# A window-ratio kernel on one core: its band matmuls split over the contraction into two of 64 rows on two row tiles

## What is computed

```python
def box_sum(x, axis, w): ...   # sum over a window of w, zero padded (w//2 before, w-w//2-1 behind)

v = _gn(x)                                    # (x - mean) / sqrt(var + 1e-5), 32 groups
s = box_sum(v, 2, 5)                          # 5 along the width
num = box_sum(s * s, 3, 20)                   # 20 along the channels
d = box_sum(box_sum(v * v, 2, 5), 3, 20)
norm = c1[None, :]                            # how many of the 5 lie inside
out = x + nan_to_num(num / (d * norm), nan=1.0)
```

## Time and profile before

| | |
|---|---|
| median of 2 runs | 423.67 us (423.52 to 423.82) |
| the profiled execution, its own time | 425.8 us |
| its span in the trace | 424.0 us |
| mean granted TensorE clock | 0.961 of full |
| TensorE matmul busy | 388.4 us (92%), 3190 instructions |
| TensorE weight loads busy | 383.7 us (90%), 3190 instructions |
| ScalarE, VectorE, GpSimd busy | 268.7, 264.8 and 233.8 us |

### The profile page before, as it was taken

How to read it: one execution, slowest core, us unless ns; L and a number is a source line. 1 busy time by engine, 2 the same in 40 slices (tenths; PEclk the granted TensorE clock), 3 DMA queues, 4 the chain that set the end, 5 groups by cost and what they waited for, 6 DMA issues and landing times. The chain is left out here.

```text
span 424.0 us, 8046 instructions
## 1 busy us (share of the span) xinstructions
PE 388.4 (92%) x3190; PEld 383.7 (90%) x3190; DVE 264.8 (62%) x427; ACT 268.7 (63%) x352; POOL 233.8 (55%) x150
## 2 busy tenths in 40 slices
PE   1995878999999999999969999999999999999983
PEld 1994878999989999999969999999999999999982
DVE  0787855666566899888877555454545555545455
ACT  1563015888887786667634676777666667767751
POOL 4000044576777777656615766666666666666531
PEclk9998685999999999999979999999999999999998
DMA  8999002088888755222220222222222222211114
GB/s 250 326 328 286 0 2 73 1 252 254 246 267 258 217 148 151 76 77 74 76 74 2 76 75 76 76 76 75 76 76 77 74 76 76 74 65 60 59 58 136
DMA packets 66485, 50.85 MB, mean 120 GB/s; under 512 B 912, under 2 KB 66448, under 8 KB 66448
## 3 DMA queue, kind: packets, MB, share of 16 engines
q1 hardware_dynamic: 66448, 50.34, 38.9%
HBM read 25.17 MB, written 25.17 MB: 119 GB/s over the span
## 5 line engine op out<-in xcount | busy, mean ns | idle before, releaser
L269 POOL TENSOR_TENSOR xs<-xs,ratio 128x768 f32<-128x768 f32 x63 | 114.6, 1819 | 120.4 <-DVE ratio L573 120.4
L263 POOL TENSOR_TENSOR xc<-xs,mean_c 128x768 f32<-128x768 f32 x64 | 117.1, 1832 | 61.6 <-DVE mean_c L519 52.2
L562 DVE SCALAR_TENSOR_TENSOR t<-D,q 128x768 f32<-128x768 f32 x64 | 61.3, 957 | 117.3 <-ACT q L352 117.2
L391 PE MATMUL D<-b_r,u 128*128 128x138 f32 (+2 forms) x768 | 105.9, 287 | 6.2 <-DVE t L562 4.9
L391 PEld LDWEIGHTS D<-b_r,u 128*128 128x128 f32 x768 | 98.2, 192 | 9.6 <-ACT u L309 4.9
L391 PE MATMUL N<-b_r,s 128*128 128x138 f32 (+2 forms) x768 | 104.8, 286 | 0.2 <-DVE ratio L573 0.2
L382 PE MATMUL U<-b5d,xc 128*128 128x128 f32 x768 | 99.4, 281 | 2.0 <-ACT xc L301 2.0
L391 PEld LDWEIGHTS N<-b_r,s 128*128 128x128 f32 x768 | 98.3, 192 | 0.4 <-issue 0.4
L382 PEld LDWEIGHTS U<-b5d,xc 128*128 128x128 f32 x768 | 94.1, 197 | 2.1 <-ACT xc L301 2.1
L346 ACT ACTIVATE q<-D 128x768 f32<-128x768 f32 x64 | 51.8, 809 | 41.9 <-PE D L391 41.9
L508 DVE BATCH_NORM_STATS2 triples<-xs 128x6 f32<-128x192 f32 (+1 forms) x192 | 64.4, 411 | 15.5 <-DMA xs<-x 15.5
(11 more groups left out here) (47 smaller groups left out, 107.9 us busy)
## 6 DMA issues: line engine op xcount, KB each, us to landing
out<-xs SPq DMA_DIRECT2D x31, 768.0 KB, 3.8
xs<-x SPq DMA_DIRECT2D x8, 1536.0 KB, 14.3
xs<-x SPq DMA_DIRECT2D x16, 768.0 KB, 6.5
out<-xs SPq DMA_DIRECT2D x2, 384.0 KB, 2.6
```

The costliest lines, as they stand in the source:

```text
L263: nc.gpsimd.tensor_tensor(pairs(xc[:, n % XC_RING, :]), pairs(x_flat(n)), mean, ALU.subtract)\
L269: nc.gpsimd.tensor_tensor(x_flat(n), x_flat(n), ratio[:, n % RATIO_RING, :], ALU.add)\
L391: mm = nc.tensor.matmul(bank[:, i, first:end], data[:, at:at + 128], b20_r[b][:, SPAN_AT[j]:SPAN_AT[j + 1]], start=j == 0, stop=j == CHUNK ...
L562: nc.vector.scalar_tensor_tensor(pairs(t1[:, :]), in_bank(D), -TINY, pairs(q[:, n % Q_RING, :]), ALU.add, ALU.mult).then_inc(t1_ready, 1)
```

## The change

Every band matmul (`box5`, `box20`) is split over its contraction, the 128 partitions, into two: rows 0 to 63 and rows 64 to 127. The two use the two 64-row tiles of the array. Since the band is narrow, each half of the rows reaches only part of the columns: 66 of 128 for the width, 73 to 83 for the channels. Two row tiles must not write one PSUM bank at the same time. So a group is computed in two halves (`half` 0 and 1): in the first, row tile 0 works on the chunks of bank 0 and row tile 1 on those of bank 1, in turn; in the second they change places. Between the halves of a group stands a half of another group, and the second half waits on a new semaphore, `half_done`, until the first has ended. To interleave the groups, the waits are taken out of them and put in front of pairs: D with U and N with S in a duo with four groups; D, U and N together in a duo with three; D and N together in the last two duos. The raw boxes are computed in pairs on all four PSUM tensors instead of two.

```diff
+        RAW_BANKS = (S, N, D, U)
...
-                bank = (S, N)[n % 2]
+                bank = RAW_BANKS[n % len(RAW_BANKS)]
...
+            HALF = 64
+            halves = [0]
+            first_half = {}
+            def tiles(bank, half):
+                if half:
+                    pe.wait_ge(half_done, first_half.pop(bank.name))
+                for j in range(CHUNKS):
+                    for t in range(2):
+                        yield j, t, (t + half) % 2
+            def keep_half(bank, half, mm):
+                if not half:
+                    halves[0] += 1
+                    first_half[bank.name] = halves[0]
+                    mm.then_inc(half_done, 1)
                 return mm
-            def box20(bank, data, b):
-                for i in range(DUO):
-                    for j, (first, end) in enumerate(SPAN):
-                        at = i * PCOLS + 128 * j
-                        mm = nc.tensor.matmul(bank[:, i, first:end], data[:, at:at + 128],
-                                              b20_r[b][:, SPAN_AT[j]:SPAN_AT[j + 1]], start=j == 0,
-                                              stop=j == CHUNKS - 1, skip_group_check=True)
+            def box5(bank, rows, weights, half):
+                for j, t, i in tiles(bank, half):
+                    chunk, at = slice(128 * j, 128 * (j + 1)), i * PCOLS + 128 * j
+                    k = slice(HALF * t, HALF * (t + 1))
+                    w0, w1 = max(HALF * t - W_LO, 0), min(HALF * (t + 1) + W_LO, W)
+                    mm = nc.tensor.matmul(bank[:, i, 128 * j + w0:128 * j + w1], rows[k, at:at + 128],
+                                          weights[k, w0:w1], start=j == 0 and half == 0, stop=half == 1,
+                                          skip_group_check=True)
+                return keep_half(bank, half, mm)
+            def box20(bank, data, b, half):
+                for j, t, i in tiles(bank, half):
+                    at = i * PCOLS + 128 * j
+                    k = slice(HALF * t, HALF * (t + 1))
+                    first = max(128 * j + HALF * t - C_HI, 0)
+                    end = min(128 * j + HALF * (t + 1) + C_LO, PCOLS)
+                    col = SPAN_AT[j] + first - SPAN[j][0]
+                    mm = nc.tensor.matmul(bank[:, i, first:end], data[k, at:at + 128],
+                                          b20_r[b][k, col:col + end - first],
+                                          start=j == 0 and half == 0, stop=half == 1, skip_group_check=True)
+                return keep_half(bank, half, mm)
...
             for n in range(TOTAL):
+                m = n + BOX_AHEAD
                 if n == 0 or n == DUOS:
                     pe.wait_ge(b20_ready, batch(n) + 1)
-                sum_d(n)
-                if n + BOX_AHEAD < TOTAL:
-                    box_u(n + BOX_AHEAD)
-                sum_n(n)
-                if n + BOX_AHEAD < TOTAL and not is_raw(n + BOX_AHEAD):
-                    box_s(n + BOX_AHEAD)
+                wait_d(n)
+                if m < TOTAL and not is_raw(m):
+                    wait_u(m)
+                    sum_d(n, 0)
+                    box_u(m, 0)
+                    sum_d(n, 1).then_inc(d_ready, 1)
+                    box_u(m, 1).then_inc(u_ready, 1)
+                    wait_n(n)
+                    wait_s(m)
+                    sum_n(n, 0)
+                    box_s(m, 0)
+                    sum_n(n, 1).then_inc(n_ready, 1)
+                    box_s(m, 1).then_inc(s_ready, 1)
+                elif m < TOTAL:
+                    wait_u(m)
+                    wait_n(n)
+                    sum_d(n, 0)
+                    box_u(m, 0)
+                    sum_n(n, 0)
+                    sum_d(n, 1).then_inc(d_ready, 1)
+                    box_u(m, 1).then_inc(u_ready, 1)
+                    sum_n(n, 1).then_inc(n_ready, 1)
+                else:
+                    wait_n(n)
+                    sum_d(n, 0)
+                    sum_n(n, 0)
+                    sum_d(n, 1).then_inc(d_ready, 1)
+                    sum_n(n, 1).then_inc(n_ready, 1)
```

More of the change, by code:

```diff
@@ L117, in window_ratio_kernel @@
         warm = sem("warm")
+        half_done = sem("half_done")
         raw_in_psum = sem("raw_in_psum")
@@ L375, in _ @@
         def _(pe):
-            def box5(bank, rows, weights):
-                for i in range(DUO):
[L380 to L383, removed]
-                return mm
-            def box20(bank, data, b):
-                for i in range(DUO):
-                    for j, (first, end) in enumerate(SPAN):
-                        at = i * PCOLS + 128 * j
-                        mm = nc.tensor.matmul(bank[:, i, first:end], data[:, at:at + 128],
-                                              b20_r[b][:, SPAN_AT[j]:SPAN_AT[j + 1]], start=j == 0,
-                                              stop=j == CHUNKS - 1, skip_group_check=True)
-                return mm
@@ L396, in box_raw @@
-            def box_raw(n):
[L398 to L404, removed]
+            HALF = 64
[7 more added lines that the diff above has]
+                        yield j, t, (t + half) % 2
@@ L406, in box_s, with wait_s @@
+            def box_raw(n):
+                for m in (n, n + 1):
+                    pe.wait_ge(loaded0[m // (STEP_DUOS * LOAD_STEPS)], 16)
+                    if m >= len(RAW_BANKS):
+                        pe.wait_ge(raw_kept, m - len(RAW_BANKS) + 1)
+                for half in range(2):
+                    for m in (n, n + 1):
+                        mm = box5(RAW_BANKS[m % len(RAW_BANKS)], x_flat(m), b5, half)
+                mm.then_inc(raw_in_psum, 2)
+            def wait_s(n):
                 pe.wait_ge(xc_ready, n + 1)
@@ L410, in box_s, with wait_u @@
                     pe.wait_ge(s2_ready, n)
-                box5(S, xc[:, n % XC_RING, :], b5).then_inc(s_ready, 1)
-            def box_u(n):
+            def wait_u(n):
                 pe.wait_ge(xc2_ready, n + 1)
@@ L417, in box_u, with wait_d @@
                     pe.wait_ge(us_ready, n)
-                box5(U, xc2[:, n % XC2_RING, :], b5d).then_inc(u_ready, 1)
-            def sum_d(n):
+            def wait_d(n):
                 pe.wait_ge(us_ready, n + 1)
@@ L424, in sum_d, with wait_n @@
                     pe.wait_ge(t1_ready, n)
-                box20(D, u[:, n % U_RING, :], batch(n)).then_inc(d_ready, 1)
-            def sum_n(n):
+            def wait_n(n):
                 pe.wait_ge(s2_ready, n + 1)
@@ L437, in sum_n, with box_s, box_u, sum_d @@
                     average_squares(1)
-                box20(N, s2[:, n % S2_RING, :], batch(n)).then_inc(n_ready, 1)
+            def box_s(n, half):
+                return box5(S, xc[:, n % XC_RING, :], b5, half)
+            def box_u(n, half):
+                return box5(U, xc2[:, n % XC2_RING, :], b5d, half)
+            def sum_d(n, half):
+                return box20(D, u[:, n % U_RING, :], batch(n), half)
+            def sum_n(n, half):
+                return box20(N, s2[:, n % S2_RING, :], batch(n), half)
             def average_means(b):
@@ L462, in _ @@
             pe.wait_ge(bands_ready, 1)
-            for n in range(RAW_DUOS):
+            for n in range(0, RAW_DUOS, 2):
                 box_raw(n)
             pe.wait_ge(b5d_ready, 1)
+            pe.wait_ge(raw_kept, RAW_DUOS)
             for k in range(WARMS):
@@ L471, in _ @@
             pe.wait_ge(mean_ready, 1)
-            pe.wait_ge(raw_kept, RAW_DUOS)
             spread_offsets().then_inc(offsets_in_psum, 1)
-            box_u(0)
-            average_squares(0).then_inc(var_in_psum, 1)
-            box_u(1)
+            wait_u(0)
+            for n in range(BOX_AHEAD):
+                if n:
+                    wait_u(n)
+                box_u(n, 0)
+                if n == 0:
+                    average_squares(0).then_inc(var_in_psum, 1)
+                box_u(n, 1).then_inc(u_ready, 1)
             pe.wait_ge(bands_ready, 2)
             for n in range(TOTAL):
+                m = n + BOX_AHEAD
                 if n == 0 or n == DUOS:
                     pe.wait_ge(b20_ready, batch(n) + 1)
-                sum_d(n)
-                if n + BOX_AHEAD < TOTAL:
-                    box_u(n + BOX_AHEAD)
-                sum_n(n)
-                if n + BOX_AHEAD < TOTAL and not is_raw(n + BOX_AHEAD):
-                    box_s(n + BOX_AHEAD)
+                wait_d(n)
[26 more added lines that the diff above has]
+                    sum_n(n, 1).then_inc(n_ready, 1)
         @block.vector
```

## The result

The changed kernel takes 752.35 us (752.33 to 752.36, 2 runs) against 423.67: 1.771 times the time before, 95% interval 1.765 to 1.778. The forecast of 490 us had the direction and was 262 us too low; the time lies inside the stated range, close to the rival "no overlap" (780 us). The experiments show that it is not that rival. The two row tiles do overlap fully. What doubled is the clock period.

A forecast was written before the change was run, and what follows sets the result against it. TensorE's weight loads were taken as the bound: 424.0 + 59.6 (raw) + 0 (steady) + 4.6 (end) + 0.5 (front) = 488.7 us of span, with 1.8 over it stated as 490. Range 455 to 790, the forecast's own 465 to 535.

The forecast's parts named there:

- no overlap: Rival: the two row tiles load weights one after the other, halves of 1.344 us, 780 us in all; chance 0.25.
- The floor of 0.112 us per pair: TensorE: each load-and-matmul pair takes at least 0.112 us for its weight load, whatever the rows or moving columns.
- Part 1: Band matmuls on two row tiles: twice the pairs, loads overlapping, 0.696 us per half, eight halves 5.57 us as now.
- The steady rounds (43): no change: The 43 rounds from duo 18 to 61 stay at 5.57 us; bounds -8 and +223 us in all.
- Part 2: The 18 raw duos: joint waits ahead of D make each round a chain, 8.1 us against 4.79, +59.6 us.
- Some rounds begin at half clock and recover in the round: Raw rounds: idle gaps of 3.4 us lower the clock at times, so 8.1 us taken between 7.6 and 10.6.
- the 10.6: Raw rounds: length in us of a round wholly at half clock; such rounds throughout would add 105 us.
- Nothing else becomes late: Steady rounds: readers of D and N end in time and half_done waits are covered, so no delay is added.
- The end +4.6: Duos 61 to 63: with both waits ahead of D, 20.9 us instead of 16.35.
- the front +0.5: Start of the kernel: first two boxes of U in halves, +0.5 us, bounds 0 and 2.
- Cheap loads: Rival: loads of a 64-row tile cost less, a half takes 0.43 us, 419 us in all; chance 0.10.

The follow-up runs named there:

- e7: Kernel before, with 64-row tiles, few columns and late waits only in duos 18 to 61, all columns in duos 28 to 33: 419.95 us, ratio 0.989.
- e10: e7 with duos 28 to 33 as in the kernel before (128-row matmuls, its order and waits): 418.94 us, ratio 0.987.
- e11: e10 with all 128 columns moved in S and U, few only in D and N: 418.77 us, ratio 0.986.
- e4: Kernel before, 128-row matmuls in its own order, moving only 66 or 83 columns after the first use of each PSUM tensor: 578.51 us.
- e9: e4 with all columns moved again in duos 28 to 33, behind the idle time at the join: 416.19 us.
- e8: Changed kernel, its order and waits, with all columns moved at the front and in duos 0 to 21 and 28 to 33: 519.22 us.
- e2: Changed kernel's order, halves and waits, but with the 128-row matmuls of before and no row tiles: 523.21 us.
- e1: Changed kernel with the same 64-row tiles, order and waits, but every matmul moves all columns of its band: 523.53 us.

## Why the prediction was wrong

- **The floor of 0.112 us per pair belongs to the weight load, and halved rows and columns don't lower it.** Right. At full clock 24 pairs of a group take 1.34 us (e7, e10, e11), and e11 shows that the columns below the floor are free.
- **Part 1, the tiles overlap; 0.696 us per half taken, 0.672 as the lower end.** Right on the overlap: 0.670 at full clock, all of it, nothing lost at the handing over. By the Trainium skill ("TensorEngine Tiling (Array Packing)", Key Properties) different tiles can execute weight loads in parallel; the traces agree (0.0557 us a pair on two tiles in e7, against 0.112 on one before). The step that failed is the clock in which it was priced: "The steady rounds (43): no change". They ran at half clock, 10.24 us instead of 5.57, and with the join and the ten duos ahead of it that is 196 us, most of the miss. I had taken for granted that a TensorE without gaps is granted the full clock. e4, e9 and e8 show that it depends on what the matmuls are: the few moving columns kept the full clock but never won it back (348 us at 0.50 in e4, 142 us at 1.00 in e9).
- **Part 2, the raw round becomes a chain through the ratio.** Right in every link (e2 has it without tiles: +75 us). "Some rounds begin at half clock and recover in the round", 8.1 us, was wrong twice. With all columns they do recover, and the average is 8.85 to 8.98 (e2, e1), so the term was too small by 0.8 us a round. With the few columns of the change no round recovered, 10.18 us, near the 10.6 that I had as the far end; that is 36 us of the miss.
- **"Nothing else becomes late" in the steady rounds.** Wrong by 0.2 us a round at full clock (e2). I had checked the readers of D and N, and not the square of xc, whose wait was moved from U to D. At the half clock of the changed kernel it costs nothing: 8 halves of 1.28 are the whole 10.24 us.
- **The end +4.6, the front +0.5.** The end came to +10.2 and the front to +21.8. Both are mostly the half clock; in e2, where it is mostly full, the end is +5.7 (20.4 against 14.7) and D of duo 0 starts 3.9 later. In before the first group of the raw boxes takes 2.90 us, the second 1.93, and from the third on they start 1.34 us apart, so the clock rose early (12.08 us); in after it never did in 51 us.
- **The rivals.** "No overlap" came nearest in time (780) and is refuted in its mechanism: it had halves of 1.344 us with the loads in turn, and the measured 1.28 are two loads at a time at half clock. Its nearness is chance. No rival had the steady rounds at half clock, though the earlier trace rows showed that a TensorE busy for all of 5.07 us can stand at 0.50. "Cheap loads" fell with e7: at full clock a pair still takes 0.111 us on its tile.
- **The range.** Its own lower end, written 465, is 471 by its own terms (424 + 49 - 8 + 4 + 2). Nothing hangs on it.

What I should have asked of the profile is whether the work that has to win the clock back is the same as before. The gaps that lose it were in the sum, and the return was not.

## What to carry to other kernels

When f32 matmuls are paced by their weight loads, splitting the contraction over two row tiles brings nothing where the columns were already below the load (S, U) and only the excess where they were above (D, N: 0.121 to 0.112); the rest of the gain must come from elsewhere. When waits are put together ahead of interleaved work, each one is a new edge in the chain, also those that looked slack: keep every wait directly ahead of the first instruction that needs it. And before matmuls are made thinner, look for each idle time ahead of them and keep some full ones behind it: here six duos with all columns were worth 162 us (e4 to e9).

## What was not expected of the hardware

- The granted clock depended on its own history. With 66 and 83 columns per load of 128, the same instructions ran for 140 us at 1.0 (e4, 73.6 to 213) and for 350 us at 0.5 after 4.07 us of idle time, the latter without a gap; six duos with all columns switched the second into the first (e9).
- Few columns also lost the full clock at a shorter idle time. About 1.5 us of it took the clock in both traces where it stood between matmuls with few columns (1.53 us ahead of D of duo 62 in e8, 1.52 ahead of D of duo 63 in e9, where the clock falls at 402.8). In the three traces with all columns there it stayed (1.53 us ahead of D of duo 62 in e1 and in e2, 1.41 ahead of D of duo 63 in the kernel before, which is at 1.00 to 421.68). No run was made to test this; the longest idle time that few columns came through at full clock is 0.75 us (e4).
- Two row tiles loaded f32 weights at the same time in every trace, though an f32 matmul sends two loads to one tile before the other tile's turn: 0.107 us per pair at half clock, 0.056 at full.
- In the raw duos of e1 and e2 a gap of about 3.3 us per round (e1: 163.0 less 103.4 us busy, e2: less 102.4, over 18 rounds) took the clock to 0.85 on average over the stretch, so the +75 us of e2's raw rounds are the wait and the clock together, and no run here prices them apart.
